# A decoder kernel: context normalised in the head, its affine on a turned copy, a gate by tanh, and part of the last stage moved into the perceiver loop

## The reference, cut to what matters

```python
x = _layernorm(x + _L0_attn_ref(x, ...))              # 1: gated delta rule, 16 heads of 8
x = _layernorm(x + _L0_xattn_ref(x, ctx_1024, ..., 16))  # 2: strided cross attention
x = _layernorm(x + _L0_ffn_ref(x, ...))               # 3: feed forward with a sine gate
x = _layernorm(x + _L1_attn_ref(x, ...))              # 4: selective state space, 256 x 16 states
x = _layernorm(x + _L1_xattn_ref(ctx_1024, x, ...))   # 5: perceiver
x = _layernorm(x + _L1_ffn_ref(x, ...))               # 6: receptance gated feed forward

# 5: both inputs are normalised, with a gain and a shift of their own
xn = _layernorm(ctx, gamma_media, beta_media)
ln = _layernorm(latents, gamma_lat, beta_lat)
q = ln @ Wq + bq
k, v = split(concatenate([xn, ln], axis=1) @ Wkv + bkv)
out = softmax(q k^T * DH ** -0.5) v     # 8 heads of 128
out @ Wo + bo

# 6: x_prev is x one token earlier
xr = mu_r * x + (1.0 - mu_r) * x_prev
xk = mu_k * x + (1.0 - mu_k) * x_prev
r = sigmoid(xr @ W_r.T)
k_act = square(relu(xk @ W_k.T))
out = r * (k_act @ W_v.T)
```

## Time and profile before

| | us |
|---|---|
| runs shown | 406.8, 404.0, 408.42 |
| their median | 406.8 |
| the profiled execution, whole | 406.31 |
| its span in the profile | 403.4 |
| busy in the span: PE, DVE, ACT, POOL | 331.6, 319.8, 210.8, 224.4 |
| stage 1, up to its output | 0 to about 100 |
| scan loop | about 157 to 290 |
| perceiver loop | about 290 to 390 |
| last normalisations and stores | about 390 to 403.4 |

### The profile page before, as it was taken

One profiled execution on the slowest core, in us unless ns is written; L12 is line 12 of the kernel. 1 busy time (PEld: TensorE's weight loads), 2 busy tenths in 40 slices (PEclk: granted clock), 3 DMA queues, 4 the chain that ended last, 5 costly groups with the idle time before them and its releaser, 6 DMA issues. The chain is left out here.

```text
span 403.4 us, 5113 instructions
## 1 busy us (share of the span) xinstructions
PE 331.6 (82%) x1578; PEld 221.6 (55%) x1578; DVE 319.8 (79%) x638; ACT 210.8 (52%) x462; POOL 224.4 (56%) x228
## 2 busy tenths in 40 slices
PE   5538748789788889779997888895899999999991
PEld 2332447787564626332433543352498877898870
DVE  1599999996877798999999899799868544754536
ACT  2642222231255669577777165663456666674650
POOL 3599899993413142779899889995502700100002
PEclk9957959999999989999999999999999999999996
DMA  8900000000000003335444434443200000000001
GB/s 267 382 30 0 0 3 1 2 1 2 0 2 0 0 2 107 95 101 160 143 139 138 150 99 126 122 137 103 61 0 1 2 0 2 1 2 2 0 0 52
DMA packets 11520, 24.52 MB, mean 61 GB/s; under 512 B 1231, under 2 KB 2255, under 8 KB 11239
## 3 DMA queue, kind: packets, MB, share of 16 engines
q1 hardware_dynamic: 11495, 24.22, 19.0%
HBM read 23.63 MB, written 0.59 MB: 60 GB/s over the span
## 5 line engine op out<-in xcount | busy, mean ns | idle before, releaser
L1057 POOL TENSOR_TENSOR arena<-arena 128x512 f32<-128x512 f32 x63 | 79.7, 1278 | 24.7 <-DVE arena L685 23.2
L685 DVE TENSOR_TENSOR_SCAN arena<-arena,ps 128x512 f32<-128x512 f32 x64 | 77.2, 1208 | 0.0
L1736 PE MATMUL ps<-arena,first_in 128*128 128x512 f32 x128 | 66.5, 603 | 5.7 <-POOL arena L1057 5.6
L1349 ACT ACTIVATE arena<-ps,arena 128x248 f32<-128x248 f32 x64 | 29.3, 463 | 41.4 <-DVE arena L716 41.4
L678 DVE TENSOR_TENSOR ps<-arena,ps 128x512 f32<-128x512 f32 x64 | 43.4, 680 | 6.0 <-PE ps L1724 5.4
L1313 ACT ACTIVATE arena<-arena,neg_a 128x508 f32<-128x508 f32 x64 | 43.2, 709 | 9.5 <-DVE arena L685 8.6
L1103 POOL TENSOR_TENSOR rstd<-veps,mhalf 128x4 f32<-128x4 f32 (+2 forms) x6 | 5.2, 860 | 74.4 <-DVE veps L782 68.3
L1570 PE MATMUL ps<-arena,first_in 128*128 128x128 f32 (+1 forms) x256 | 31.7, 286 | 12.8 <-POOL arena L916 12.8
L1570 PEld LDWEIGHTS ps<-arena,first_in 128*128 128x128 f32 x256 | 30.7, 201 | 14.1 <-issue 8.1
L1724 PE MATMUL ps<-arena,pick_wide 96*128 96x512 bf16 x64 | 24.5, 385 | 12.9 <-DVE arena L685 12.8
L1736 PEld LDWEIGHTS ps<-arena,first_in 128*128 128x128 f32 x128 | 23.3, 191 | 20.7 <-POOL arena L1057 12.8
(11 more groups left out here) (285 smaller groups left out, 815.4 us busy)
## 6 DMA issues: line engine op xcount, KB each, us to landing
arena<-c_rows_dram SPq DMA_DIRECT2D x64, 256.0 KB, 3.2
fold_in<-in_fold_dram SPq DMA_DIRECT2D x1, 2056.0 KB, 15.0
late_in<-in_late_dram SPq DMA_DIRECT2D x1, 1422.5 KB, 18.4
early_in<-in_early_dram SPq DMA_DIRECT2D x1, 921.5 KB, 9.3
xres<-in_x_dram SPq DMA_DIRECT2D x1, 512.0 KB, 6.2
rows_in<-in_rows_dram SPq DMA_DIRECT2D x1, 512.0 KB, 15.9
kv_ctx<-in_context_dram SPq DMA_DIRECT2D x1, 480.0 KB, 11.0
first_in<-in_first_dram SPq DMA_DIRECT2D x1, 465.0 KB, 3.8
```

Source lines behind the costliest of these rows:

```text
L685: nc.vector.tensor_tensor_scan(hist[:, q % NBUF], fade[:, q % NFADE], chain(q), 0.0, ALU.mult, ALU.add).then_inc(S("scan"), 1)
L1057: tt(seen[:, q % NBUF], hist[:, q % NBUF], c_wide[:, q % NBUF], ALU.mult).then_inc(S("read_out"), 1)
L1349: act(s5_p[:, u % 2, h], sim_bank(u)[:, h * 256:h * 256 + KV], ACT.Exp, bias=s5_max[:, u % 2, h:h + 1], accum_out=s5_den[:, u % 2, h:h + 1 ...
L1736: mm(y_bank, ident, seen[:, p % NBUF], start=False, stop=p % NS == NS - 1).then_inc(S("seen_used"), 1)
```

## The change

- Loads: the order is first, context, fold, early, x, rows, late. g_med and be_med move from rows (one copy per partition of a row of channels) to late (one value per partition, channels on the partitions).
- Context statistics: the eight bn_stats, eight bn_aggr and the addition of eps move on DVE to the copies of the first projections, two bn_stats before the last copy and the rest behind it. rstd is now a square root on ACT, between the roots of K and Q, and a reciprocal on DVE, with the product for the bias, between the normalisations of K and Q; POOL's three small operations go.
- Context normalisation: ACT's eight activations move from q = NK4 + 4, 5 to stage 1, ahead of the widening of pick.
- Affine: POOL's media goes. PE turns the normalised context in iterations q = 28, 29, ACT copies it to kvT with gain and shift at q = 29, 30, PE turns that copy back at q = 31, 32, and ACT copies the result into kv_ctx at q = 32, 33. The turning at NK4 + 18, 19 goes.
- Gate of stage 6: sigmoid(r) = 0.5 (1 + tanh(r / 2)); ACT uses Tanh with scale 0.5, without the table load, DVE forms (t + 1) k and then x + 0.5 of it, with two scalar_tensor_tensor in place of two tensor_tensor.
- Perceiver loop: mix6(0) at k = 23, out6(0) at k = 25, square6(0) at 24, the gate of part 0 at 25; DVE's gated residual of part 0 at 27, its statistics at 28, its normalisation at 29. After the loop DVE does the residuals of parts 1 and 2, then their statistics, then their normalisations. ORDER and normed() follow.

```diff
--- before.py
+++ after.py
@@ -47,19 +47,21 @@
              ("b_in", 2 * NH), ("w_x", NH * 2 * NS), ("w_dt", NH * DI), ("b_dt", NH), ("w_out", NH * D),
-             ("a_log", NH * NS), ("d_skip", NH), ("b_x", 1), ("g_lat", 1), ("be_lat", 1),
+             ("a_log", NH * NS), ("d_skip", NH), ("b_x", 1), ("g_lat", 1), ("be_lat", 1), ("g_med", 1), ("be_med", 1),
              ("w_r", D), ("w_k", D), ("w_v", D), ("mu_r", 1), ("mu_k", 1),
 }
-ROWS = ["bo0", "b2", "b_out", "bo1", "g_med", "be_med", "g_lat", "be_lat"]
+ROWS = ["bo0", "b2", "b_out", "bo1", "g_lat", "be_lat"]
 RIDES = {
-    "k_ps": ("square", 2),
+    "ctx_root": ("square", 2),
+    "k_ps": ("square", 3),
+    "ctx_back": ("v_turned", 1),
     "kend_ps": ("norm_root", 2),
     "w_ps": ("qkv_even", B // 2),
-    "mean_rstd": ("ctx_rstd", 1),
+    "mean_rstd": ("gate_factor", 1),
     "inverse5": ("ctx_var", 1),
@@ -139,12 +141,14 @@
         PARTS = [(0, HB), (HB, B - 1), (B - 1, B)]
-        ORDER = [(1, 0), (1, 1), (2, 0), (2, 1), (3, 0), (3, 1), (4, 0), (4, 1), (5, 0), (5, 1), (5, 2), (6, 0), (6, 1), (6, 2)]
+        ORDER = [(1, 0), (1, 1), (2, 0), (2, 1), (3, 0), (3, 1), (4, 0), (4, 1), (5, 0), (6, 0), (5, 1), (5, 2), (6, 1), (6, 2)]
                 return 3 * B + k + (HB if n == 7 else 0) + (HB if k > HB else 0)
+            if n == 5 and k > HB or n == 6 and k <= HB:
+                return 5 * B + HB + k
             return {1: 0, 2: B, 3: 2 * B, 5: 5 * B, 6: 6 * B}[n] + k
@@ -277,6 +281,7 @@
         NU = 4 * B
+        CTX_BANKS = (4, 6)
         folded = [tiles["fold"][:, k * HW:(k + 1) * HW] for k in range(4)]
@@ -336,10 +341,10 @@
             sp.dma_start(tiles["first"][:, soon:], first[:, soon:]).then_inc(S("second_in"), 16)
-            sp.dma_start(xres[:], x).then_inc(S("x_in"), 16)
-            sp.dma_start(tiles["early"][:], early).then_inc(S("early_in"), 16)
             sp.dma_start(kv_ctx[0:TC], context).then_inc(S("ctx_in"), 16)
             sp.dma_start(tiles["fold"][:], fold).then_inc(S("fold_in"), 16)
+            sp.dma_start(tiles["early"][:], early).then_inc(S("early_in"), 16)
+            sp.dma_start(xres[:], x).then_inc(S("x_in"), 16)
             sp.dma_start(row_in[:], rows.partition_broadcast(P)).then_inc(S("rows_in"), 16)
@@ -423,6 +428,17 @@
                 nc.vector.tensor_copy(qkvt[:, :, b], bank(b)[:, 0:3 * D + 2 * H].rearrange("p (n h) -> p n h", h=H)).then_inc(S("qkv_odd"), 1)
+                if b == B - 3:
+                    ve.wait_ge(S("ctx_in"), 16)
+                    for i in range(2):
+                        step(nc.vector.bn_stats(cstats[0:TC, i], kv_ctx[0:TC, i]))
+            for b in range(2, B):
+                step(nc.vector.bn_stats(cstats[0:TC, b], kv_ctx[0:TC, b]))
+            join()
+            for b in range(B):
+                step(nc.vector.bn_aggr(cmv[0:TC, b], cstats[0:TC, b]))
+            join()
+            ts(cveps[0:TC], cmv[0:TC, :, 1], EPS, None, ALU.add).then_inc(S("ctx_var"), 1)
@@ -434,6 +450,10 @@
                 h = slice(n * T, (n + 1) * T)
+                if n:
+                    ve.wait_ge(*after("ctx_root", 1))
+                    then(nc.vector.reciprocal(crstd[0:TC], crstd[0:TC]))
+                    stt(cmean_rstd[0:TC], cmv[0:TC, :, 0], -1.0, crstd[0:TC], ALU.mult, ALU.mult).then_inc(S("ctx_rstd"), 1)
                 ve.wait_ge(S("norm_root"), n + 1)
@@ -633,15 +653,6 @@
             rectified(3)
-
-            ve.wait_ge(S("ctx_in"), 16)
-            for b in range(B):
-                step(nc.vector.bn_stats(cstats[0:TC, b], kv_ctx[0:TC, b]))
-            join()
-            for b in range(B):
-                step(nc.vector.bn_aggr(cmv[0:TC, b], cstats[0:TC, b]))
-            join()
-            ts(cveps[0:TC], cmv[0:TC, :, 1], EPS, None, ALU.add).then_inc(S("ctx_var"), 1)
@@ -790,9 +801,9 @@
                 ve.wait_ge(S("kv_mm"), last)
-                then(tt(gate6[:, h], gate6[:, h], bank(key6[part])[:, 0:(last - first) * T], ALU.mult))
-                then(tt(xrow[:, 0, first:last], xrow[:, 1, first:last],
-                        gate6[:, h].rearrange("p (b c) -> p b c", c=D), ALU.add))
+                then(stt(gate6[:, h], gate6[:, h], 1.0, bank(key6[part])[:, 0:(last - first) * T], ALU.add, ALU.mult))
+                then(stt(xrow[:, 0, first:last], gate6[:, h].rearrange("p (b c) -> p b c", c=D), 0.5,
+                         xrow[:, 1, first:last], ALU.mult, ALU.add))
@@ -821,16 +832,22 @@
                     finish5(0)
+                if k == 27:
+                    gated_residual(0)
+                if k == 28:
+                    variances6(0)
+                if k == 29:
+                    finish6(0)
             finish5(1)
             finish5(2)
-            for part in range(len(PARTS)):
-                gated_residual(part)
-                variances6(part)
-                if part:
-                    finish6(part - 1)
-            finish6(part)
+            gated_residual(1)
+            gated_residual(2)
+            variances6(1)
+            variances6(2)
+            finish6(1)
+            finish6(2)
@@ -980,10 +997,6 @@
             residual_half(4, 0, row_in[:, ROWS.index("b_out")])
-            po.wait_ge(S("ctx_var"), 1)
-            then(tt(crstd[0:TC], cveps[0:TC], mhalf[0:TC], ALU.pow))
-            then(ts(cmean_rstd[0:TC], cmv[0:TC, :, 0], -1.0, None, ALU.mult))
-            tt(cmean_rstd[0:TC], cmean_rstd[0:TC], crstd[0:TC], ALU.mult).then_inc(S("ctx_rstd"), 1)
@@ -1027,17 +1040,6 @@
                 tt(lat_rstd[:, h], lat_rstd[:, h], mhalf[:, h], ALU.pow).then_inc(S("lat_rstd"), 1)
-
-            def media(part):
-                if part == 0:
-                    po.wait_ge(S("ctx_norm"), B)
-                    po.wait_ge(S("rows_in"), 16)
-                    step(tt(kv_ctx[0:TC], kv_ctx[0:TC],
-                            row_in[0:TC, ROWS.index("g_med")].unsqueeze(1).to_broadcast([TC, B, D]), ALU.mult))
-                else:
-                    join()
-                    tt(kv_ctx[0:TC], kv_ctx[0:TC], row_in[0:TC, ROWS.index("be_med")].unsqueeze(1).to_broadcast([TC, B, D]),
-                       ALU.add).then_inc(S("kv_ctx"), 1)
@@ -1070,10 +1072,6 @@
                     latent_scale(0)
-                if q == NK4 + 11:
-                    media(0)
-                if q == NK4 + 13:
-                    media(1)
                 if q == NK4 + 16:
@@ -1134,6 +1132,9 @@
                 act(norm2[n], norm2[n], ACT.Sqrt).then_inc(S("norm_root"), 1)
+                if n == 0:
+                    ac.wait_ge(S("ctx_var"), 1)
+                    act(crstd[0:TC], cveps[0:TC], ACT.Sqrt).then_inc(S("ctx_root"), 1)
@@ -1143,6 +1144,11 @@
                 act(fold_qk[:, 4 * g:4 * g + 4], bank(6 + g).rearrange("p (h c) -> p h c", h=4), ACT.Copy).then_inc(S("fold_qk"), 1)
+
+            ac.wait_ge(S("ctx_rstd"), 1)
+            for b in range(B):
+                act(kv_ctx[0:TC, b], kv_ctx[0:TC, b], ACT.Identity, bias=cmean_rstd[0:TC, b:b + 1],
+                    scale=crstd[0:TC, b:b + 1]).then_inc(S("ctx_norm"), 1)
@@ -1419,15 +1425,20 @@
                     table_of(ACT.Exp)
+                if q in (29, 30):
+                    k = q - 29
+                    ac.wait_ge(S("ctxT5_mm"), HB * (k + 1))
+                    act(kvT[:, k * HB:(k + 1) * HB, 0:TC], bank(CTX_BANKS[k]).rearrange("p (b t) -> p b t", b=HB)[:, :, 0:TC],
+                        ACT.Identity, bias=W("be_med"), scale=W("g_med")).then_inc(S("kvT_ctx"), 1)
+                if q in (32, 33):
+                    k = q - 32
+                    ac.wait_ge(*after("ctx_back", HB * (k + 1)))
+                    act(kv_ctx[0:TC, k * HB:(k + 1) * HB], bank(CTX_BANKS[k])[0:TC].rearrange("p (b c) -> p b c", b=HB),
+                        ACT.Copy).then_inc(S("kv_ctx"), 1)
                 if q == NK4 + 3:
                     act(fold_bo[:], bank(5)[:, D:2 * D], ACT.Copy).then_inc(S("fold_bo_sum"), 1)
-                if q in (NK4 + 4, NK4 + 5):
-                    ac.wait_ge(S("ctx_rstd"), 1)
-                    for b in range((q - NK4 - 4) * HB, (q - NK4 - 3) * HB):
-                        act(kv_ctx[0:TC, b], kv_ctx[0:TC, b], ACT.Identity, bias=cmean_rstd[0:TC, b:b + 1],
-                            scale=crstd[0:TC, b:b + 1]).then_inc(S("ctx_norm"), 1)
                 if q == NK4 + 8:
@@ -1442,11 +1453,6 @@
                     query_out(0, q - NK4 - 13)
-                if q in (NK4 + 19, NK4 + 20):
-                    k = q - NK4 - 19
-                    ac.wait_ge(S("ctxT5_mm"), HB * (k + 1))
-                    act(kvT[:, k * HB:(k + 1) * HB, 0:TC], bank(4 + k).rearrange("p (b t) -> p b t", b=HB)[:, :, 0:TC],
-                        ACT.Copy).then_inc(S("kvT_ctx"), 1)
                 if q in (NK4 + 21, NK4 + 22):
@@ -1477,10 +1483,11 @@
-            def sigmoid6(part):
+            def tanh6(part):
                 first, last = PARTS[part]
                 ac.wait_ge(S("r6_mm"), last)
```

(42 more changed lines are left out.)

## The result

| | before | after |
|---|---|---|
| median of the runs, us | 406.11 (404.0 to 408.42, 4 runs) | 400.43 (399.52 to 400.56, 4 runs) |
| ratio after to before, 95% interval | | 0.9862 (0.9825 to 0.9899) |
| span of the profiled execution, us | 403.4 | 397.1 |

The change makes the kernel 5.7 us faster, 1.4%. The forecast was 403.8 with a range of 400.8 to 407.0: the sign was on the less likely side of its chances (0.31 for faster by over 1%) and the time lies 0.4 us under the range.

What follows compares the result with a forecast made beforehand. DVE was taken to set the scan's pace and PE to bound the perceiver. Terms 0.35 - 2.2 + 0.5 - 1.6 = -2.95 us, rounded to -3.0, gave 403.8 us from 406.8, range 400.8 to 407.0.

Steps and rivals of the forecast that it cites:

- The step that failed: Scan's second gate_first on DVE: claimed to keep its long form of 3.57 us, since DVE and POOL both come earlier.
- The first rival: Scan: lighter POOL lets DVE's gate_first in at a boundary, another 2.5 us gone, 401.3 us; chance 0.17.
- Head: Between normalising K and Q on DVE: new reciprocal, wait and small operation delay Q, +0.35 us.
- Waits of PE for POOL: Scan: without POOL's two affine blocks, two waits of PE go, 2 x 0.90 = 1.8 us gained.
- Turning of the context: Scan: four PE transposes leave the steps at 263.56 and after, one of two on the path, 0.4 us gained.
- The 16 transposes: Scan steps 28, 29, 31 and 32: transposes added on PE, counted as 0 us (bounds 0 and 0.5).
- Perceiver: Perceiver loop: DVE's added residual, statistics and normalisation reach PE through mixed_out, +0.5 us (bounds 0.2 and 1.2).
- Tail: After the last projection: part 0's DVE work has left, last normalisation ends earlier, -1.6 us (bounds -1.2 and -2.0).
- The second: Head: POOL's multiplication shuts out DVE's new small operation, Q 1.9 us later, 405.7 us; chance 0.12.
- The third: Scan: first gate_first also shut out, 2.76 us, with the head's 1.9 making +4.7, 408.5 us; chance 0.05.
- The fourth: Scan: no gain, PE already the limit in query steps and POOL still late, 406.0 us; chance 0.12.
- The fifth: Perceiver and tail: tanh needs table loads beside exp, about 3.5 us, 407.3 us; chance 0.04.

Runs made afterwards that it cites:

- edit 3: Kernel before, with POOL's affine of the context (gain and shift) cut to two of 1024 columns; 402.46 us, ratio 0.9898.
- edit 6: Kernel after, with the last stage's part 0 moved back to its old places, residual, statistics and normalisation behind the loop, tanh kept; 401.02 us, ratio 0.9895.
- edit 8: Kernel after, with Sigmoid in place of Tanh on ACT, so the gate's value differs; 402.88 us, one execution.
- edit 9: Kernel after, with DVE's three pieces for part 0 moved from units 27 to 29 into its idle gap behind the loop; 398.97 us, ratio 0.9848.
- edit 4: Kernel after, with two 120x1024 POOL multiplications on an unread tile added where the affine had been; 404.75 us, ratio 0.9985.
- edit 5: Kernel after, with the two added POOL multiplications of edit 4 and POOL's residual (4,1) two queries later; 405.56 us, one execution.
- edit 1: Kernel before, unchanged, profiled a second time; 405.58 us, one execution.
- edit 7: Kernel before, with only the perceiver and tail part of the change, nothing in head or scan; 404.14 us, ratio 0.9952.
- edit 2: Kernel before, with POOL's residual (4,1) two queries later; 404.56 us, ratio 0.9937.
- edit 10: Edit 9, with two queries four and five steps later and their evictions, a softplus, the folding of bo and residual (4,1) moved to match; 397.93 us, ratio 0.9806.
- edit 11: Edit 10, with DVE's two small head operations and ACT's eight context normalisations placed later; 400.07 us, ratio 0.9866.

## Why the prediction failed, step by step

**The step that failed** is the one about gate_first: "DVE comes 2.1 us earlier but POOL too, and the same run of products and residual lies before it, so I assume the long form again." The first half is right. DVE came 269.56 - 267.23 = 2.33 us earlier, and POOL's product 268.84 - 266.44 = 2.40. The second half, "the same run", is wrong. In before POOL is behind the scan and works from 241.9 us to 272.59 without a pause. Its product of step 52 starts 0.16 us after that step's scan has ended (265.00 + 1.21 = 266.21, timeline of before, DVE and POOL):

```profile
265.00 1.21 DVE L685 TENSOR_TENSOR_SCAN arena<-arena,ps 128x512 f32<-128x512 f32 x1
...
266.37 1.28 POOL L1057 TENSOR_TENSOR arena<-arena 128x512 f32<-128x512 f32 x1
```

Without the affine POOL has caught up. In after and in edits 3, 6, 8 and 9 it waits for DVE's scan before this product (0.16 us at 263.98 in the rows of edit 6), and starts it 0.08 us after the scan's end (262.69 + 1.21 = 263.90). From there to the gate both engines do the same work in all these kernels. So the product beside the gate stands 0.80 us ahead of it where POOL has caught up, 0.72 in before, and 0.32 where POOL is loaded further. The prediction never asked whether POOL would still be behind, though it took the relief of POOL as the scan's gain. All cases in order of that head start:

| kernel | product ahead of the gate, us | residual behind the products | gate, us |
|---|---|---|---|
| edit 4, POOL loaded | 0.32 | yes | 3.98 |
| edit 5, loaded, residual later | 0.32 | no | 2.73 |
| before; edit 1; edit 7 | 0.72; 0.71; 0.73 | yes | 3.57; 3.56; 3.55 |
| edit 2, residual later | 0.73 | no | 1.09 |
| after; edits 3, 6, 8, 9 | 0.79 to 0.81 | yes | 1.01 to 1.02 |
| edits 10, 11 | 0.79 to 0.80 | no | 1.02 |
| the first gate, all kernels | 0.98 to 1.01 | other work | 0.81 to 0.82 |

At 0.79 or more the gate is let in whatever is behind, at 0.32 it isn't, and at 0.72 the residual decides. Orders that were traced more than once came out the same within 0.02 us; edits 2, 4 and 5 have one trace each. That relieving POOL makes the gate short is shown by edits 3 and 4, and that the residual decides in before's case by edit 2. That the head start as such decides is not shown: it was never moved by itself, and in every short case with the residual behind, POOL had also paused within the last 4 us, while in every long one it had worked without a pause for 25 us and more. The rule by which the chip chooses stays open.

The first rival was this case, with -2.5 us against -2.56 measured; what was wrong was its chance. I gave it 0.17 on the ground that the surroundings stay the same. Its price off my own range of 402.3 to 405.4 gives 399.8 to 402.9, which holds the measured 400.43; the stated range stopped at 400.8. (The 0.31 for faster by over 1% was also added up a little high: 0.17 and a fifth to a quarter of 0.50 are 0.27 to 0.30.)

**The terms of the sum.** Head: +0.35 forecast, +0.31 measured. Context statistics, ACT's normalisations, the table: 0 and 0, with 0.48 and 3.12 us of cover left (0.4 and 2.9 in the prediction). Waits of PE for POOL: -1.8, shown alone by edit 3 (-1.80) and in reverse by edit 4 (+1.73). Its ground for stopping at 1.93 us a step, that PE itself is the limit in six steps, holds in after, but edit 10 shows that POOL's earlier lateness is behind that too in four of them. Turning of the context: -0.4; step 51 to 52 is 1.94 instead of 2.35 us, which gives 0.41. The 16 transposes: 0 forecast; scan step 33 to 34 takes 1.77 instead of 1.71 and nothing else in 28 to 36 changes by more than 0.01, so +0.06. Perceiver: +0.5 forecast, +0.46 measured, by edits 6, 7 and 9, with the three additions within 0.03 us of their sizes each. It reaches PE through mixed_out, as said: the projection at 378.52 waits 0.58 us for it, the one that answers it in edit 9 (377.83) 0.33, as in before. Tail: -1.6 forecast, -1.78 measured; it was mis-sized by 0.2, since the last normalisation started at 8.07 us after the last projection and took 1.24, against 9.46 - 1.34 = 8.12 and 1.34 in my count.

**What no term had.** 0.17 us before the first square sum and 0.38 us between head and scan. In the second stretch the executions of all these kernels, which have the same work there or nearly so, range from 124.82 to 127.40 us, and the granted clock isn't the same in them: from 40 to 100 us it was 0.91 in before and 0.94 in after. Before and after stand at 126.55 and 126.17. The first square sum comes anywhere from 15.05 to 16.53 us in them. So these 0.55 us, a tenth of the gain, are within what one execution differs from another, and I put no cause of the change to them; that the forecast missed them is no fault of its mechanism.

**The other rivals.** The second did not occur (0.17 us at 20.48), by 0.06 us, nearly as reckoned; that was close enough to call it luck. Its price of 1.9 is for the worst meeting: edit 11 shows 0.6 for the same exclusion when the operation comes 1.05 us into a POOL operation of 1.79. The third did not occur: the first gate took 0.82, and its head start of 1.00 us was as in before. The fourth is refuted by edit 3. The fifth did not occur, and edit 8 gives its price as 2.65 us, not 3.5.

## What to carry to other kernels

Where an operation of VectorE on two SBUF inputs stands beside an unbroken run of GpSimd, take its time as one of several values, the end of each GpSimd operation of that run with 0.55 us behind it, work out the next and the last, and give neither much less than the other as soon as the change shifts either engine's queue by a tenth of a microsecond. Ask above all whether GpSimd will still be behind or will have caught up; look also for what can be moved out from behind it, as one line of order was worth 0.6% here. Price a relief of GpSimd by the waits that others have for it and not by the work removed (2 x 2.35 us of its work went, 1.8 us of waits came back, and 2.56 more by the exclusion). And put operations that are moved under a busy engine where the other one's longest idle row is: the same three additions cost 0.46 us in the ring and nothing in the gap of 5.58 us. And ask of an experiment's gain where in the trace it lies: edit 10's lay ahead of the queries that it was meant to test.

## What the runs showed of the hardware

- Exclusion between VectorE and GpSimd works in both directions in these traces. The Trainium skill (GPSIMD Engine Reference, Specifications) has the contention of GpSimd with VectorE instructions on two SBUF inputs; the traces agree, and add what it costs. A multiplication of 128x512 takes 0.69 us with GpSimd idle and 0.81 to 3.98 beside it, and in all these traces ended about 0.55 us after the end of a GpSimd operation. When it is let in between two GpSimd multiplications, the second of these takes longer: the two take 2.94 to 2.96 us instead of 2.49 to 2.53. In the head a VectorE multiplication of 128x1024 took 2.05 us where it began 0.93 us ahead of GpSimd's, which then took 2.95, and 3.04 where it began 0.01 us behind it, and GpSimd's took 1.97.
- A VectorE operation that waits can be passed over: with GpSimd's queue full it wasn't let in at the first end of a GpSimd operation (2.73 us in edit 5) or at the first two (3.55 to 3.98 us). The length repeats from execution to execution, 3.57, 3.56 and 3.55 us in three traces and 1.01 to 1.02 in seven.
- A table load took 1.28 us each of three times in edit 8, and 68% and 71% of it were paid where ScalarE had some idle time around it. The one of before, at 389.08, was hidden whole.
